# A router inside an attention loop: row normalising moved to ScalarE, and two largest, masks, ranks and sends moved between the slots of a hand-written pipeline

## The chip, the cores and the metric

One core of a Trainium2 chip runs the whole program in one launch. The metric is the device time of an execution in microseconds. The inputs are those of the reference with seed 0, in float32.

## What is computed

Two layers over x of shape (8, 512, 128), each with an adaptive layer norm (shift, scale and gate per sequence). The first has a Mamba-2 mixer and a capacity-limited mixture of experts (here no expert is kept, so its branch isn't entered). The second, whose stages this document is about, is attention with one head and then a router with 8 experts:

```python
mod = (_silu(L1_c) @ L1_wmod).reshape(L1_c.shape[0], 6, 1, -1)
...
h = _layernorm(x) * (1 + ca) + sa
x = x + ga * _L1_attn_ref(h, ...)
h = _layernorm(x) * (1 + cb) + sb
x = x + gb * _L1_ffn_ref(h, ...)

def _L1_ffn_ref(tgt, Wr, br, W1, b1, W2, b2, gamma, beta):
    logits = jnp.einsum('bsd,ed->bse', tgt, Wr) + br
    top_v, top_i = jax.lax.top_k(logits, 2)
    top_w = jax.nn.softmax(top_v, axis=-1)
    ...
    h = jax.nn.relu(jnp.einsum('bsd,efd->bsef', tgt, W1) + b1)
    o = jnp.einsum('bsef,edf->bsed', h, W2) + b2
    tgt2 = jnp.einsum('bsed,bse->bsd', o, router_w)
    return _layer_norm(tgt + tgt2, gamma, beta)
```

## The kernel before, in words

The program has three parts in time. The mixer of layer 0 runs first. The attention of layer 1 with its router follows, and its first slots run beside the mixer's last. Then 71 tiles of 128 queued rows go through their expert, results are scattered back, and the final norm writes the output. The change touches the second part only.

**Slots.** The 8 sequences are 32 chunks of 128 tokens. Each engine has a function `body(m, b, c, first)` that is called for m from -9 to 37, with b = m // 4 and c = m % 4. What a slot m contains, and in which order, is written out by hand in each engine's body; every engine runs its own list in order, and semaphores tie the lists together. In slot m, TensorE (engine PE in the rows) turns the exponentials of chunk m+1 (L1699), makes the scores of chunk m+3 (L1693) and the product with the values of chunk m (`attend`, L1710). ScalarE (ACT) copies the turned exponentials (L1338) and takes exp of the scores (L1342). VectorE (DVE) takes the row maximum of chunk m+3 (nmx, L1471), the reciprocal (rinv, L1483), adds the result to x (L1493), and takes its statistics (L1496, L1507). Once per sequence come query, key and value products (L1675, L1679, L1685), their evictions (the values with an addition on DVE, L1502, in slots with c = 0) and two small weight products on DVE (wvg and bvg, L1466 and L1467, c = 1).

**The router's way of a pair.** Two chunks are a group; there are 16 groups, and group q ends in slot E = 2q + 1, always odd. A group's way through the engines is spread over later slots:

- slot E: variance plus epsilon (ve_b, DVE L1512), then the power -0.5 on GpSimd (POOL, rs_b, L1287; "the pow" from here on);
- slot E+1: the normalised rows (x - mean) * rs_b, two passes of 128x128 on DVE (L1518);
- slot E+2: TensorE turns them (L1718), ScalarE applies scale and shift (h4, L1361);
- slot E+3: TensorE makes rows and logits (L1725), DVE adds the bias (lg), finds the two largest (top) and their indices (top_i), makes the masks (mk, L1535), their sum (ms), the running counts (base) and the weights (wa, L1545 and after); ScalarE takes exp of the difference (eexp, L1367) and copies the rows out twice (L1370, L1371);
- slot E+4: ranks on TensorE (L1735, L1737), which need ms and base;
- slot E+5: rank plus queue start, times masks, summed to the queue numbers (pos, L1487) on DVE, and the sends: four indirect DMAs per group from POOL (L1265), each of 128 rows.

POOL's body issues the sends of a slot first and the pow of that slot second:

```python
for q, j in scatters_at.get(m, ()):
    ...
    scatter(q, j)
if m in ends_at:
    ...
    wait(pool, "b_ve", q + 1)
    wait(pool, "b_xn", q)
    g.tensor_tensor(rs_b[:, 0:n], ve_b[:, 0:n], k.half_neg[:, 0:n], ALU.pow).then_inc(S["b_rs"], 1)
```

`scatter` waits for the group's numbers (`q_pos`) and weights (`q_w1`). After the last slot a matmul counts the queues, DVE builds the table of tiles (L1556 to L1569), and the experts begin once the table is there and all sends have landed.

Of the kernel before, what the change touches and what calls it, by code (L numbers as in the profile page):

```python
# [10 lines left out]
P = 128  # L11
# [104 lines left out]
def mixer(nc, k, a):  # L116
# [6 lines left out]
    with ExitStack() as rounded:  # L123
# [544 lines left out]
        def tensor_program(pe):  # L668
# [153 lines left out]
            "d_hi", "d_t", "d_bd")] + [("c_cu", 1), ("c_mm", 2), ("c_row_mm", 1), ("c_gate", 5), ("c_rk", 1), ("w_mul", NTAP), ("w_hi", NTAP + 2)]  # L822
# [193 lines left out]
def layer1(nc, k, a, out, mixer_of, kept):  # L1016
# [10 lines left out]
            "q_mr", "q_pos", "q_wa", "q_w0", "q_w1", "q_lg", "f_cnt"))  # L1027
# [4 lines left out]
    with ExitStack() as ctx:  # L1032
# [5 lines left out]
        st_b = sb("st_b", [P, 2, 6]); mv_b = sb("mv_b", [P, 2, NC, 2]); ve_b = sb("ve_b", [P, NC]); rs_b = sb("rs_b", [P, NC])  # L1038
# [104 lines left out]
        for m in range(BEGIN, END):  # L1143
            b, c = m // NC, m % NC
            if c == 0 and seq(b + 1):
                used(("v", b + 1), "u_dve")
            if c == 2 and seq(b + 2):
                used(("q", b + 2), "u_act")
            if c == 3 and seq(b + 2):
                used(("k", b + 2), "u_act")  # L1150
            if m - 2 in ends_at:
                used(("h4", ends_at[m - 2]), "u_act")
            if m - 3 in ends_at:
                used(("row", ends_at[m - 3]), "u_act")
            if m - 4 in ends_at:
                used(("rank", ends_at[m - 4]), "u_dve")
# [9 lines left out]
        totals |= {n: G for n in ("b_ve", "b_rs", "b_xn", "q_diff", "q_exp", "q_ms", "q_mr", "q_pos", "q_wa", "q_w0", "q_w1", "q_lg")}  # L1166
# [11 lines left out]
        def filled(e, key):  # L1178

            wait(e, "u_mm", use[key][0] + 1)  # L1180
# [142 lines left out]
        def _(act):  # L1323
            ac = nc.scalar

            def body(m, b, c, first):
                if m == BEGIN:
                    act.wait_ge(S["aw_in"], 16 * 11)
                    wait(act, "sc_mm", 2)
                    ac.activation(wvT[:], bank[0][:, 0:P], ACT.Copy)  # L1330
                    ac.activation(bvT[:], bank[0][:, P:2 * P], ACT.Copy).then_inc(S["sc_exp"], 1)
                    wait(act, "f_mm", k.ends["conv"])
                    wait(act, "res_x", NB)
                    ac.activation(eexp[:, 0:1], ones[:, 0:1], ACT.Exp)
                n = m + 1
                if chunk(n):
                    wait(act, "p_t", n + 1)
                    ac.activation(pt[:, n % 3, :], bank[5][:], ACT.Copy).then_inc(S["p_act"], 1)  # L1338
                n = m + 3
                if chunk(n):  # L1340
                    wait(act, "sc_max", n + 1)
                    ac.activation(pr[:, n % 3, :], bank[3 + n % 2][:], ACT.Exp, bias=nmx[:, n % 2:n % 2 + 1], accum_out=sm[:, n % 4:n % 4 + 1]).then_inc(S["sc_exp"], 1)  # L1342
                if c == 2 and seq(b + 2):
                    s = b + 2
                    filled(act, ("q", s))
                    if s == 0:
                        wait(act, "a_set", 1)
                    ac.activation(qT[:, s % 2, :], bank_of(("q", s))[:], ACT.Identity, scale=0.125, bias=bq[:]).then_inc(S["u_act"], 1)
                if c == 3 and seq(b + 2):
                    s = b + 2  # L1350
                    filled(act, ("k", s))
                    ac.activation(kT[:, s % 2, :], bank_of(("k", s))[:], ACT.Identity, bias=k.attn_b[:, 1:2]).then_inc(S["u_act"], 1)
                if m - 2 in ends_at:
                    q = ends_at[m - 2]
                    s, _, n = groups[q]
                    filled(act, ("h4", q))
                    if q >= 2:
                        filled(act, ("row", q - 2))
                    elif first:
                        wait(act, "s_yz", NT)  # L1360
                    ac.activation(h4[:, q % 2, 0:n * P], bank_of(("h4", q))[:, 0:n * P], ACT.Identity, scale=mod[:, 1, 4, s:s + 1], bias=mod[:, 1, 3, s:s + 1]).then_inc(S["u_act"], 1)  # L1361
                if m - 3 in ends_at:
                    q = ends_at[m - 3]
                    s, c0, n = groups[q]
                    wait(act, "q_diff", q + 1)
                    wait(act, "q_w1", q)
                    ac.activation(eexp[:, 0:n], ediff[:, 0:n], ACT.Exp).then_inc(S["q_exp"], 1)  # L1367
                    filled(act, ("row", q))
                    src = rows_in(q, n)[:, :, 0:P]
                    ac.activation(row[:, s * NC + c0:s * NC + c0 + n, 0, 0:D], src, ACT.Copy)  # L1370
                    ac.activation(row[:, s * NC + c0:s * NC + c0 + n, 1, 0:D], src, ACT.Copy).then_inc(S["u_act"], 1)  # L1371
# [60 lines left out]
        def _(dve):  # L1432
# [8 lines left out]
            def body(m, b, c, first):  # L1441
# [42 lines left out]
                if m - 5 in ends_at:  # L1484
# [35 lines left out]
                if m - 3 in ends_at:  # L1520
                    q = ends_at[m - 3]
# [11 lines left out]
                    wait(dve, "q_at", done)  # L1533
                    for i in range(2):
                        v.tensor_tensor(mk[:, q % 2, i, 0:n], top_i[:, 0:n, i:i + 1].broadcast_to([P, n, NE]), over_chunks(k.iota[:], n), ALU.is_equal).then_inc(S["q_mask"], 1)  # L1535
                    wait(dve, "q_mask", 2 * (q + 1))
                    v.tensor_tensor(ms[:, 0:n], mk[:, q % 2, 0, 0:n], mk[:, q % 2, 1, 0:n], ALU.add).then_inc(S["q_ms"], 1)
                    wait(dve, "q_ms", q + 1)
                    if q == 0:
                        wait(dve, "a_set", 1)  # L1540
                    for i in range(n):
                        wait(dve, "q_base", at + i)
                        v.tensor_tensor(base[:, q % 2, i + 1, :] if i + 1 < n else base[:, (q + 1) % 2, 0, :], base[:, q % 2, i, :], ms[:, i, :], ALU.add).then_inc(S["q_base"], 1)
# [125 lines left out]
        def _(pe):  # L1669
            t_ = nc.tensor  # L1670

            def query(s, first):
                if first and s == 0:
                    wait(pe, "s_aev", k.next_ready[s])
                t_.matmul(bank_of(("q", s))[:], wq, h_next[:, s, :], start=True, stop=True).then_inc(S["u_mm"], 1)  # L1675
# [63 lines left out]
            def body(m, b, c, first):  # L1739
# [24 lines left out]
                if chunk(m + 3):  # L1764
                    scores(m + 3)
                if chunk(m):
                    attend(m)
# [10 lines left out]
                if m - 4 in ends_at:  # L1778
                    ranks(ends_at[m - 4])
# [144 lines left out]
```

## Time and profile before

| | us |
|---|---|
| median of 3 runs | 572.94 (572.18 to 574.33) |
| the profiled execution | 574.9 |
| its span, first to last instruction | 573.0 |
| TensorE busy in the span | 507.9 (89%) |
| DVE busy | 438.5 (77%) |
| ScalarE busy | 352.2 (61%) |
| POOL busy | 280.6 (49%) |

Busy shares are means over the whole program. Matmuls are pipelined and their ends are modelled. POOL's row in the timeline shows an indirect DMA as the time POOL is held by issuing it, not as the transfer. "Idle before" in brackets names what the profile infers as the releaser; a wait for several semaphores is put down to the one that came last by the profile.

### The profile page before, as it was taken

The numbers are of one execution on the slowest core, as the hardware profiler recorded it, in microseconds if no ns is written. First come the engines' busy times: TensorE is split into PE (matmuls) and PEld (weight loads), VectorE is DVE, ScalarE is ACT, GpSimd is POOL, SyncE is SP. The second block draws the span as 40 slices with busy tenths as digits, with TensorE's granted clock in tenths as the row PEclk, the third lists the DMA queues.
The fourth block names the chain that finished last, engine by engine and source line by source line (L and its number), as shares of the span: only waits on it lengthen the run. The fifth ranks groups of instructions, "written<-read, shape, count | busy, mean of one in ns | idle before, by whom it ended". The sixth has DMA issues, their size and how long they took to land.

```text
span 573.0 us, 12147 instructions
## 1 busy us (share of the span) xinstructions
PE 507.9 (89%) x3328; PEld 420.9 (73%) x3328; DVE 438.5 (77%) x1651; ACT 352.2 (61%) x944; POOL 280.6 (49%) x349
## 2 busy tenths in 40 slices
PE   5799999999999999988999999515999999999991
PEld 3467888888888887756777777414999999989630
DVE  3758898989898989977899999853666666656375
ACT  3978787787878584544656666312566666555354
POOL 3144363535353535410266666770666666666323
PEclk9989999999999999999999999855999999999996
DMA  9299999999100000006511111111122222222293
GB/s 279 85 290 176 178 165 179 165 173 185 61 19 15 6 18 2 21 18 194 152 44 39 39 38 44 44 58 45 57 72 68 76 72 68 61 72 67 80 278 112
DMA packets 76386, 54.70 MB, mean 95 GB/s; under 512 B 10524, under 2 KB 69408, under 8 KB 76184
## 3 DMA queue, kind: packets, MB, share of 16 engines
q1 hardware_dynamic: 70352, 43.39, 38.4%
q0 software_dynamic: 4320, 8.99, 4.7%
q10 hardware_dynamic: 1640, 1.45, 0.8%
q8 instruction: 32, 0.52, 0.4%
q14 instruction: 42, 0.34, 0.2%
HBM read 40.62 MB, written 31.58 MB: 126 GB/s over the span
## 4 chain that ended last, share of the span: by engine, by line
PE 62%; DVE 22%; ACT 6%; issue 5%; DMA 2%; DVEq 1%; SPq 0%; POOL 0%; ACTq 0%
PE bank L1817 10%; PE bank L1834 10%; PE bank L678 5%; PE bank L680 5%; PE bank L679 5%; PE bank L789 4%; DVE nmx L1471 2%; PE bank L724 2%; PE bank L809 2%; PE bank L735 2%; PE bank L785 2%; PE bank L794 2%; PE bank L1710 2%; PE bank L720 1%; DVE arena L1607 1%
## 5 line engine op out<-in xcount | busy, mean ns | idle before, releaser
L1307 POOL DMA_INDIRECT results<-arena x71 | 74.2, 1045 | 60.6 <-ACT arena L1395 55.7
L1817 PE MATMUL bank<-front,arena 128*128 128x128 f32 x568 | 77.9, 281 | 2.7 <-DVE arena L1607 1.4
L1265 POOL DMA_INDIRECT queue<-arena,pos x64 | 62.6, 979 | 28.1 <-issue 14.1
L1834 PE MATMUL bank<-h_all,front 128*128 x568 | 75.7, 277 | 0.1
L1817 PEld LDWEIGHTS bank<-front,arena 128*128 128x128 f32 x568 | 70.6, 195 | 5.7 <-issue 4.5
L292 POOL TENSOR_TENSOR arena<-arena,half_neg 128x1 f32<-128x1 f32 x32 | 19.7, 616 | 110.2 <-ACT arena L458 110.2
L1834 PEld LDWEIGHTS bank<-h_all,front 128*128 128x128 f32 x568 | 69.6, 193 | 0.3 <-issue 0.2
L1607 DVE COPY arena<-arena 128x516 f32 x71 | 36.6, 515 | 40.4 <-issue 37.3
L1389 ACT ACTIVATE front<-bank 128x128 f32<-128x128 f32 x71 | 19.7, 278 | 60.9 <-PE bank L1810 42.9
L678 PE MATMUL bank<-h_hi,wc_hi 128*128 128x512 f32 x96 | 45.1, 470 | 1.3 <-ACT arena L439 1.3
L1618 DVE TENSOR_SCALAR front<-bank,arena 128x128 f32<-128x128 f32 x142 | 42.8, 342 | 2.9 <-PE bank L1817 2.6
L1408 ACT ACTIVATE front<-bank,arena 128x128 f32<-128x128 f32 x142 | 43.2, 353 | 2.1 <-PE bank L1817 2.1
L1710 PEld LDWEIGHTS bank<-front 128*128 128x128 f32 x256 | 33.4, 192 | 13.9 <-issue 13.4
L679 PE MATMUL bank<-h_hi,wc_lo 128*128 128x512 f32 x96 | 38.9, 405 | 0.0
L514 DVE TENSOR_TENSOR_SCAN arena<-bank,arena 128x512 f32<-128x512 f32 x32 | 38.8, 1213 | 0.0
L680 PE MATMUL bank<-h_lo,wc_hi 128*128 128x512 f32 x96 | 38.7, 404 | 0.0
L1342 ACT ACTIVATE arena<-bank,nmx 128x512 f32<-128x512 f32 x32 | 22.1, 690 | 23.9 <-DVE nmx L1471 22.3
L1395 ACT ACTIVATE arena<-arena 128x128 f32<-128x128 f32 x71 | 28.5, 402 | 13.0 <-DVE arena L1625 5.2
L789 PEld LDWEIGHTS bank<-arena 128*128 128x128 f32 x256 | 33.1, 192 | 2.5
L789 PE MATMUL bank<-arena 128*128 128x64 f32 x256 | 34.1, 262 | 0.0
L1710 PE MATMUL bank<-front 128*128 128x128 f32 x256 | 33.7, 275 | 0.0
L1810 PE MATMUL bank<-ident_wr,arena 128*128 128x128 f32 x71 | 19.9, 280 | 15.1 <-DMA arena<-queue 15.1
(295 smaller groups left out, 1393.1 us busy)
## 6 DMA issues: line engine op xcount, KB each, us to landing
queue<-in_pad_rows SPq DMA_DIRECT2D x8, 2178.0 KB, 34.8
arena<-queue SPq DMA_DIRECT2D x71, 66.0 KB
rows<-mod_rows SPq DMA_DIRECT2D x8, 384.0 KB, 6.3
x_keep<-x SPq DMA_DIRECT2D x8, 256.0 KB, 2.3
arena<-in_w SPq DMA_DIRECT2D x1, 2048.0 KB, 9.1
h_all<-in_w SPq DMA_DIRECT2D x1, 2048.0 KB, 7.9
h_all<-results SPq DMA_DIRECT2D x8, 256.0 KB, 4.8
arena<-results SPq DMA_DIRECT2D x8, 256.0 KB, 5.2
```

The lines of the kernel that those rows point to most:

```text
L678: t_.matmul(dst, l_hi, r_hi, start=first, stop=False)
L679: t_.matmul(dst, l_lo, r_hi, start=False, stop=False)
L680: return t_.matmul(dst, l_hi, r_lo, start=False, stop=last)
L789: mm = t_.matmul(bank[5][:, h * HD:h * HD + HD], mt[:, t % 2, h * P:h * P + P], xdt[:, t % 2, h * HD:h * HD + HD], start=False, stop=True, ...
L1265: pool.indirect_dma_start(k.queue, bass.IndirectOffsetOnAxis(ap=pos[:, s, i, c0 + j:c0 + j + 1], axis=0), row[:, s * NC + c0 + j, i, :], N ...
L1307: pool.indirect_dma_start(k.results, bass.IndirectOffsetOnAxis(ap=xg[:, c, D:D + 1].bitcast(I32), axis=0), yw[:, c, :], None).then_inc(S[f ...
L1408: ac.activation(ht[:, p, g * P:g * P + P], bank[2 + p][:, g * P:g * P + P], ACT.Relu, bias=wc[:, p, FF + g:FF + g + 1]).then_inc(S["ht_a"], 1)
L1607: v.tensor_copy(wc[:, p, :], w1[:, e, :]).then_inc(S["w_cp"], 1)
L1618: v.tensor_scalar(ht[:, p, g * P:g * P + P], bank[6 + p][:, g * P:g * P + P], wc[:, p, FF + g:FF + g + 1], 0.0, ALU.add, ALU.max).then_inc ...
L1710: mm = t_.matmul(bank[6 + n % 2][:, 0:D], pt[:, n % 3, i * P:i * P + P], vv[:, s % 2, i, :], start=(i == 0), stop=(i == NC - 1))
L1817: mm = t_.matmul(bank[(2 if g < NG // 2 else 6) + p][:, g * P:g * P + P], wc[:, p, g * P:g * P + P], xt[:, p, :], start=True, stop=True)
L1834: mm = t_.matmul(bank[4 + p][:, 0:D], ht[:, p, g * P:g * P + P], w2[:, e, g, :], start=(g == 0), stop=(g == NG - 1))
```

## The change

Every step of a group's way from slot E+1 on changes its place, its engine, or both:

- the normalised rows are made on ScalarE, at the end of slot E+1, as x * rs_b + nm_b; DVE makes nm_b = -mean * rs_b for it in the same slot, right behind the row maximum;
- TensorE turns the rows in slot E+2 as before, but ahead of `attend`, and makes rows and logits at the end of that same slot E+2, not in E+3;
- DVE adds the bias and finds the two largest and the indices in slot E+2 (before E+3), and makes masks, ms and base early in slot E+3 (before: late in E+3) and the weights at its end;
- on ScalarE, eexp comes first in slot E+3, h4 and the copies behind the copy of the turned exponentials;
- ranks move from E+4 to E+3, numbers and sends from E+5 to E+4;
- the loop has one slot less, the new semaphore takes another retired one's place, and the list `use`, by which three PSUM banks go round, follows the new order.

The diff, cut to what the text speaks of:

```diff
         for q, (s, c0, n) in enumerate(groups):
             for j in range(n):
-                at = max(at + (1.0 if n == NC else 0.75), end_of[q] + 5)
+                at = max(at + 0.75, end_of[q] + 4)
                 scatters_at.setdefault(int(at), []).append((q, j))
-        BEGIN, END = -9, NT + 6
+        BEGIN, END = -9, NT + 5
...
         # ScalarE
+                if m - 3 in ends_at:
+                    q = ends_at[m - 3]
+                    n = groups[q][2]
+                    wait(act, "q_diff", q + 1)
+                    wait(act, "q_w1", q)
+                    ac.activation(eexp[:, 0:n], ediff[:, 0:n], ACT.Exp).then_inc(S["q_exp"], 1)
                 n = m + 1
                 if chunk(n):
                     wait(act, "p_t", n + 1)
                     ac.activation(pt[:, n % 3, :], bank[5][:], ACT.Copy).then_inc(S["p_act"], 1)
...
+                if m - 1 in ends_at:
+                    q = ends_at[m - 1]
                     s, c0, n = groups[q]
+                    if q >= 1:
+                        filled(act, ("h4", q - 1))
+                    wait(act, "b_nm", q + 1)
+                    for i in range(n):
+                        ins = ac.activation(xn_b[:, i, :], x[:, s * NC + c0 + i, :], ACT.Identity, scale=rs_b[:, i:i + 1], bias=nm_b[:, i:i + 1])
+                    ins.then_inc(S["b_xn"], 1)
...
         # DVE, behind the row maximum
+                if m - 1 in ends_at:
+                    q = ends_at[m - 1]
+                    s, c0, n = groups[q]
+                    wait(dve, "b_rs", q + 1)
+                    v.scalar_tensor_tensor(out=nm_b[:, 0:n], in0=mv_b[:, s % 2, c0:c0 + n].rearrange("p c t -> p (c t)")[:, 0::2], scalar=-1.0, in1=rs_b[:, 0:n],
+                                           op0=ALU.mult, op1=ALU.mult).then_inc(S["b_nm"], 1)
+                if m - 3 in ends_at:
...
+                    for i in range(2):
+                        v.tensor_tensor(mk[:, q % 2, i, 0:n], top_i[:, 0:n, i:i + 1].broadcast_to([P, n, NE]), over_chunks(k.iota[:], n), ALU.is_equal).then_inc(S["q_mask"], 1)
...
-                if m - 5 in ends_at:
-                    q = ends_at[m - 5]
+                if m - 4 in ends_at:
+                    q = ends_at[m - 4]
                     s, c0, n = groups[q]
                     filled(dve, ("rank", q))
...
         # DVE, at the slot's end
-                if m - 1 in ends_at:
-                    q = ends_at[m - 1]
-                    s, c0, n = groups[q]
-                    wait(dve, "b_rs", q + 1)
-                    for i in range(n):
-                        ins = v.tensor_scalar(xn_b[:, i, :], x[:, s * NC + c0 + i, :], mv_b[:, s % 2, c0 + i, 0:1], rs_b[:, i:i + 1], ALU.subtract, ALU.mult)
-                    ins.then_inc(S["b_xn"], 1)
-                if m - 3 in ends_at:
-                    q = ends_at[m - 3]
+                if m - 2 in ends_at:
+                    q = ends_at[m - 2]
...
         # TensorE
                 if chunk(m + 3):
                     scores(m + 3)
+                if m - 2 in ends_at:
+                    hidden_rows(ends_at[m - 2])
                 if chunk(m):
                     attend(m)
...
                 if m - 2 in ends_at:
-                    hidden_rows(ends_at[m - 2])
+                    rows_and_logits(ends_at[m - 2])
                 if m - 3 in ends_at:
-                    rows_and_logits(ends_at[m - 3])
-                if m - 4 in ends_at:
-                    ranks(ends_at[m - 4])
+                    ranks(ends_at[m - 3])
```

POOL's body stands as it was. Its order changes through the table of sends, here at the first groups (rs_b is the pow, queue the sends). Before:

```order
L292 TENSOR_TENSOR arena<-arena,half_neg 128x1
L278 TENSOR_TENSOR arena<-arena,half_neg 128x1 x2
L1277 MEMSET arena 128x64x2
L1287 TENSOR_TENSOR rs_b<-ve_b,half_neg 128x2 x3
L1265 DMA queue<-arena,pos 34816x132 x4
L1287 TENSOR_TENSOR rs_b<-ve_b,half_neg 128x2
```

And in the changed kernel:

```order
L292 TENSOR_TENSOR arena<-arena,half_neg 128x1
L278 TENSOR_TENSOR arena<-arena,half_neg 128x1 x2
L1277 MEMSET arena 128x64x2
L1287 TENSOR_TENSOR rs_b<-ve_b,half_neg 128x2 x2
L1265 DMA queue<-arena,pos 34816x132 x4
L1287 TENSOR_TENSOR rs_b<-ve_b,half_neg 128x2
```

From there on four sends and a pow alternate in both. The sends of group q stand ahead of the pow of group q + 3 before, and ahead of that of group q + 2 in the change; eight sends stand at the end, not twelve.

DVE in the loop before, from a group's numbers (pos) on, in an even slot:

```order
L1487 TENSOR_REDUCE pos<-mr 128x2x2
L1493 SCALAR_TENSOR_TENSOR x<-bank,rinv,x 128x128
L1496 BN_STATS st_b<-x 128x6
L1507 BN_AGGR mv_b<-st_b 128x2
L1518 TENSOR_SCALAR arena<-x,mv_b,rs_b 128x128 x2
L1525 TENSOR_TENSOR lg<-bank,br 128x16
L1528 MAX top<-lg 128x8 x2
L1530 TENSOR_TENSOR ediff<-top 128x2
L1532 MAX_INDEX top_i<-top,lg 128x8 x2
L1535 TENSOR_TENSOR mk<-top_i,iota 128x16 x2
```

And in the changed kernel, from pos, now in an odd slot, into the next even one:

```order
L1521 TENSOR_REDUCE pos<-mr 128x2x2
L1527 SCALAR_TENSOR_TENSOR x<-bank,rinv,x 128x128
L1530 BN_STATS st_b<-x 128x6
L1541 BN_AGGR mv_b<-st_b 128x2
L1546 TENSOR_SCALAR ve_b<-mv_b 128x2
L1552 TENSOR_TENSOR lg<-bank,br 128x16
L1555 MAX top<-lg 128x8 x2
L1557 TENSOR_TENSOR ediff<-top 128x2
L1559 MAX_INDEX top_i<-top,lg 128x8 x2
L1482 TENSOR_REDUCE nmx<-bank 128x1
L1487 SCALAR_TENSOR_TENSOR nm_b<-mv_b,rs_b 128x2
L1495 TENSOR_TENSOR mk<-top_i,iota 128x16 x2
```

The two passes that read rs_b are gone from DVE; in their place nm_b reads it, and masks, x and the rest of the even slot stand behind nm_b.

## Rows read from the trace of the kernel before

**Rows 1.** Windows, all engines: us, busy us (instructions), granted TensorE clock, DMA share, GB/s.
```profile
285.97:356.00 70.03, 66.75 (x419) 50.40 (x417) 64.71 (x344) 42.05 (x109) 46.55 (x51) 1.00 0.12 40
356.00:378.00 22.00, 12.49 (x77) 9.83 (x77) 17.67 (x111) 8.07 (x23) 16.86 (x18) 0.78 0.15 48
378.00:394.00 16.00, 0.92 (x2) 0.36 (x2) 6.19 (x20) 0.47 (x2) 6.71 (x7) 0.50 0.18 51
```

**Rows 2.** Timeline of DVE, two pairs of slots: start us, duration us, line, out<-in.
```profile
303.12 0.19 DVE L1487 TENSOR_REDUCE pos<-mr 128x4 int32<-128x32 f32 x1
...
303.92 0.67 DVE L1502 TENSOR_TENSOR front<-bank,bvg 128x512 f32<-128x512 f32 x1
...
306.08 0.26 DVE L1535 TENSOR_TENSOR mk<-top_i,iota 128x16 f32<-128x16 uint32 x2
...
306.86 0.16 DVE L1545 TENSOR_SCALAR wa<-eexp 128x2 f32<-128x2 f32 x1
...
307.36 0.29 DVE L1466 TENSOR_TENSOR wvg<-wvo,rows 128x128 f32<-128x128 f32 x1
...
307.77 0.68 DVE L1471 TENSOR_REDUCE nmx<-bank 128x1 f32<-128x512 f32 x1
308.37 0.15 DVE L1483 RECIPROCAL rinv<-sm 128x1 f32<-128x1 f32 x1
...
309.28 0.18 DVE L1507 BATCH_NORM_AGGREGATE mv_b<-st_b 128x2 f32<-128x6 f32 x1
...
309.57 0.69 DVE L1471 TENSOR_REDUCE nmx<-bank 128x1 f32<-128x512 f32 x1
...
310.67 0.19 DVE L1487 TENSOR_REDUCE pos<-mr 128x4 int32<-128x32 f32 x1
...
311.57 0.58 DVE L1518 TENSOR_SCALAR arena<-x,mv_b,rs_b 128x128 f32<-128x128 f32 x2
...
317.23 0.19 DVE L1487 TENSOR_REDUCE pos<-mr 128x4 int32<-128x32 f32 x1
```

**Rows 3.** Timeline of POOL, the same stretch; idle time before in brackets.
```profile
304.09 1.03 POOL L1265 DMA_INDIRECT queue<-arena,pos  x1 [0.97 <-DVE x L1493]
...
307.95 0.96 POOL L1265 DMA_INDIRECT queue<-arena,pos  x1 [0.30 <-issue]
309.75 0.72 POOL L1287 TENSOR_TENSOR rs_b<-ve_b,half_neg 128x2 f32<-128x2 f32 x1 [0.84 <-DVE ve_b L1512]
```

**Rows 4.** Timeline of TensorE, the same stretch.
```profile
306.69 0.17 PE L1735 MATMUL bank<-ms,tri_b 128*128 128x16 bf16 x1 [0.30 <-issue]
...
307.17 0.63 PE L1699 MATMUL bank<-ident_wr,arena 128*128 128x128 f32 x4 [0.19 <-ACT front L1338]
307.64 1.02 PE L1693 MATMUL bank<-front 128*128 128x512 f32 x2
```

**Rows 5.** ScalarE's line 366, an affine pass of the same shape.
```profile
L366 ACT ACTIVATE arena<-x,arena x32: 477/486/500, 6.9 to 167.4; 128x128 f32<-128x128 f32 x32
```

**Rows 6.** Timeline: first number row on DVE, and the tail, all engines.
```profile
282.52 0.19 DVE L1487 TENSOR_REDUCE pos<-mr 128x4 int32<-128x32 f32 x1
...
370.67 0.76 POOL L1287 TENSOR_TENSOR rs_b<-ve_b,half_neg 128x2 f32<-128x2 f32 x1
370.96 0.19 DVE L1487 TENSOR_REDUCE pos<-mr 128x4 int32<-128x32 f32 x1
...
389.20 0.20 DVE L1569 CAST tile_at<-tile_r 128x72 int32<-128x72 f32 x1
```

**Rows 7.** Timeline of TensorE at an early stall.
```profile
23.09 0.39 PE L680 MATMUL bank<-h_lo,wc_hi 128*128 128x512 f32 x1
25.89 0.66 PE L762 MATMUL bank<-ident_wr,arena 128*128 128x128 f32 x4 [2.41 <-ACT arena L358]
```

**Rows 8.** Windows after that stall.
```profile
27.00:28.00 1.00, 0.11 (x1) 0.12 (x1) 0.75 (x1) 0.97 (x3) 0.00 (x0) 0.52 0.74 237
33.00:34.00 1.00, 1.00 (x4) 0.77 (x4) 0.47 (x1) 0.59 (x2) 1.00 (x2) 0.57 1.06 421
```

More of the change, by code:

```diff
@@ L1037, in layer1 @@
         st_a = sb("st_a", [P, NC, 6]); mv_a = sb("mv_a", [P, NC, 2]); ve_a = sb("ve_a", [P, NC]); rs_a = sb("rs_a", [P, NC])
-        st_b = sb("st_b", [P, 2, 6]); mv_b = sb("mv_b", [P, 2, NC, 2]); ve_b = sb("ve_b", [P, NC]); rs_b = sb("rs_b", [P, NC])
+        st_b = sb("st_b", [P, 2, 6]); mv_b = sb("mv_b", [P, 2, NC, 2]); ve_b = sb("ve_b", [P, NC]); rs_b = sb("rs_b", [P, NC]); nm_b = sb("nm_b", [P, NC])
         front = k.front
@@ L1151, in layer1 @@
             if m - 2 in ends_at:
-                used(("h4", ends_at[m - 2]), "u_act")
+                used(("row", ends_at[m - 2]), "u_act")
             if m - 3 in ends_at:
-                used(("row", ends_at[m - 3]), "u_act")
-            if m - 4 in ends_at:
-                used(("rank", ends_at[m - 4]), "u_dve")
+                used(("rank", ends_at[m - 3]), "u_dve")
             if m == 2:
@@ L1338, in body @@
                     ac.activation(pt[:, n % 3, :], bank[5][:], ACT.Copy).then_inc(S["p_act"], 1)
+                if m - 2 in ends_at:
+                    q = ends_at[m - 2]
+                    s, _, n = groups[q]
+                    filled(act, ("h4", q))
+                    if q >= 2:
+                        filled(act, ("row", q - 2))
+                    elif first:
+                        wait(act, "s_yz", NT)
+                    ac.activation(h4[:, q % 2, 0:n * P], bank_of(("h4", q))[:, 0:n * P], ACT.Identity, scale=mod[:, 1, 4, s:s + 1], bias=mod[:, 1, 3, s:s + 1]).then_inc(S["u_act"], 1)
+                if m - 3 in ends_at:
+                    q = ends_at[m - 3]
+                    s, c0, n = groups[q]
+                    src = rows_in(q, n)[:, :, 0:P]
+                    ac.activation(row[:, s * NC + c0:s * NC + c0 + n, 0, 0:D], src, ACT.Copy)
+                    ac.activation(row[:, s * NC + c0:s * NC + c0 + n, 1, 0:D], src, ACT.Copy).then_inc(S["u_act"], 1)
                 n = m + 3
@@ L1471, in body @@
                     v.tensor_reduce(nmx[:, n % 2:n % 2 + 1], bank[3 + n % 2][:], AX.X, ALU.max, negate=True).then_inc(S["sc_max"], 1)
-                if m - 5 in ends_at:
-                    q = ends_at[m - 5]
+                if m - 1 in ends_at:
+                    q = ends_at[m - 1]
+                    s, c0, n = groups[q]
+                    wait(dve, "b_rs", q + 1)
+                    v.scalar_tensor_tensor(out=nm_b[:, 0:n], in0=mv_b[:, s % 2, c0:c0 + n].rearrange("p c t -> p (c t)")[:, 0::2], scalar=-1.0, in1=rs_b[:, 0:n],
+                                           op0=ALU.mult, op1=ALU.mult).then_inc(S["b_nm"], 1)
+                if m - 3 in ends_at:
+                    q = ends_at[m - 3]
+                    s, c0, n = groups[q]
+                    at, done = s * NC + c0, s * NC + c0 + n
+                    wait(dve, "q_at", done)
+                    for i in range(2):
+                        v.tensor_tensor(mk[:, q % 2, i, 0:n], top_i[:, 0:n, i:i + 1].broadcast_to([P, n, NE]), over_chunks(k.iota[:], n), ALU.is_equal).then_inc(S["q_mask"], 1)
+                    wait(dve, "q_mask", 2 * (q + 1))
+                    v.tensor_tensor(ms[:, 0:n], mk[:, q % 2, 0, 0:n], mk[:, q % 2, 1, 0:n], ALU.add).then_inc(S["q_ms"], 1)
+                    wait(dve, "q_ms", q + 1)
+                    if q == 0:
+                        wait(dve, "a_set", 1)
+                    for i in range(n):
+                        wait(dve, "q_base", at + i)
+                        v.tensor_tensor(base[:, q % 2, i + 1, :] if i + 1 < n else base[:, (q + 1) % 2, 0, :], base[:, q % 2, i, :], ms[:, i, :], ALU.add).then_inc(S["q_base"], 1)
+                if m - 4 in ends_at:
+                    q = ends_at[m - 4]
                     s, c0, n = groups[q]
@@ L1483, in body @@
                     v.reciprocal(rinv[:, n % 2:n % 2 + 1], sm[:, n % 4:n % 4 + 1]).then_inc(S["p_rinv"], 1)
-                if m - 5 in ends_at:
+                if m - 4 in ends_at:
+                    q = ends_at[m - 4]
+                    s, c0, _ = groups[q]
                     wait(dve, "q_mr", q + 1)
@@ L1532, in body @@
                         v.max_index(top_i[:, i, :], top[:, i, :], lg4[:, i, :]).then_inc(S["q_at"], 1)
[L1533 to L1543, printed above, removed]
+                if m - 3 in ends_at:
+                    q = ends_at[m - 3]
+                    s, c0, n = groups[q]
+                    at, done = s * NC + c0, s * NC + c0 + n
                     wait(dve, "q_exp", q + 1)
```

30 lines of the change are left out of this document (8 added, 22 removed).

## The prediction, made before the changed kernel had run

> **What bounds the kernel now.** The windows come first [rows 1], because shares of the whole span hide the stages. From 286 to 356 us, the attention loop, TensorE is busy 66.75 of 70.03 us and DVE 64.71; the rest of DVE is pieces of some 0.04 us between dependent instructions. Then, from 356 to 394 us, TensorE runs dry (12.49 of 22.00 us, then 0.92 of 16.00): this is the router's tail, its last groups, the sends that are left, the tile table.
>
> The timelines say who sets the pace of the loop. DVE goes from one pair of slots to the next without a real wait; four slots take 14.11 us from the queue numbers at 303.12 to those at 317.23 [rows 2]. TensorE waits for DVE at one place per four slots, the rank matmul and what follows it, 0.30 and 0.19 us [rows 4]. So DVE bounds the loop and TensorE is 0.5 us behind.
>
> The third reading decides the case: POOL [rows 3]. A group's four sends start 0.78 us after its queue numbers end (303.31 to 304.09), run back to back at 1.26 us, and end at 308.91, 4.82 us later. POOL executes in order. The next pow (line 1287) waits behind them, and here costs nothing: it starts at 309.75, when DVE's variance is ready, and ends at 310.47, while DVE asks for it at 311.57 [rows 2]. The sends fit into the stretch between a group's numbers, early in an even slot, and the variance, late in the odd slot after it.
>
> **The change part by part.**
>
> *Sends and pow on POOL.* Numbers and sends move from the fifth slot after a group's end to the fourth. Groups end in odd slots, so the fourth is odd too, and it is the slot of the pow of the group two further on. POOL's body issues sends first and pow second. The order of POOL says so: two pows and not three ahead of the first four sends. And on DVE the first reader of that pow is now the shift nm_b, right behind the row maximum of the next slot, ahead of the masks, of x and of everything that TensorE waits for. Behind pos stand four sends on POOL, and on DVE only some 2.4 us of work before nm_b (worked out below). That closes a ring once per pair of slots:
> - pos to pow ready: 0.78 + 4.82 + 0.05 (issue) + 0.72 = 6.37 us [rows 3].
> - rest of the even slot from nm_b: nm_b 0.16 (taken as the small pass at 306.86), masks, sum and base 0.78 (306.08 to 306.86), weights 0.50 (to 307.36), reciprocal to aggregate 0.91 (308.37 to 309.28) and 0.10 until the next: 2.45 us [rows 2].
> - the odd slot until pos ends: 309.57 to 310.86, 1.29 us [rows 2].
>
> Sum 10.11 us. With the values' addition (0.67, some 0.6 of it its own) and the two weight products (307.36 to 307.77, 0.41) it is 11.1 in one pair of two. Four slots: 21.2 us instead of 14.1. DVE's own work in them is 14.11 less 0.4 a pair (below), 13.3 us, of which 2 x (2.45 + 1.29) + 1.0 = 8.5 is in the ring; the other 4.8, 2.4 a pair, lies between pos and nm_b beside POOL's 6.37. So DVE stands 3.9 to 4.0 us at nm_b in each pair.
>
> From the first pos to the fourteenth are 13 such steps: 13 x 10.11 = 131.4, plus five values 3.0, plus four weight products 1.6, less two slots without a row maximum 1.2: 134.8 us. Before, that was 370.96 - 282.52 = 88.4 us [rows 6]. **+46.4.**
>
> *The start.* The first pos comes a slot sooner. An odd slot's maximum starts 1.80 us ahead of the next even slot's (307.77 and 309.57 [rows 2]), and two groups' normalising, some 0.5 us each on DVE, is gone from in front of it: **-2.8.**
>
> *The tail.* In the trace the last pow ends at 371.43, 0.28 us after the fourteenth pos (371.15) [rows 6]. Now it stands behind four sends, at +6.37: 6.1 later. What follows it is the old chain with the same links: rows, turning, affine pass, logits, two largest, masks, ranks, numbers, table, to 389.40. Only its first link is slower, see next. Of the eight sends that are left, the first starts some 3 us behind that pow (nm_b, masks and numbers of group 14, 2.2, and 0.78), so they end near 3 + 8 x 1.26 = 13 us; the table ends at 389.40 - 371.43 = 18.0, and stays last unless a send takes over 4 us to land. **+6.4.**
>
> *Normalising on ScalarE.* Two DVE passes of 0.58 us together [rows 2] become two on ScalarE; the nearest row there, same shape, from x with scale and shift, shows 0.49 each [rows 5]: 0.35 us more in the link, counted in the tail. In the loop ScalarE is busy 42.05 of 70.03 us [rows 1] and all of it lies beside POOL's sends. If that cover were gone it would matter: ScalarE gets 0.97 us more per pair and h4, copies and weights in another order, up to 0.9 us for a pair if the rows came after TensorE wants them. The Trainium skill (ScalarE: Activation LUTs, Rules for kernel authors) says to do products and sums on VectorE, not on ScalarE, which speaks against this part. By that rule each of 16 pairs would be dearer, 16 x 0.35 = 5.6 us; by the rows it is a price in the last pair alone.
>
> *What DVE saves.* 0.50 us of normalising less 0.1 of nm_b and a shorter wait at the masks, 0.4 to 0.5 us per pair, is what the change frees where DVE bounds. DVE does not bound any more: the saving is in the ring already and else only lengthens the standing at nm_b. TensorE's moves (turning before attend, logits a slot sooner, ranks a slot sooner) each issue the same matmuls; their waits fall into the 3.9 us too.
>
> Sum without the clock: 46.4 - 2.8 + 6.4 = **+50.0 us.**
>
> *TensorE's clock.* It is at 2.4 GHz throughout the loop now [rows 1]. With 6.7 us of work in 10.1 or 11.1, TensorE gets a gap of 3.4 to 4.4 us per pair, ahead of the ranks. A gap of that size is in the trace: matmuls end at 23.48, 0.66 us of them come at 25.89 [rows 7], and the granted clock of 27 to 28 us is 0.52, half; it is back within 33 to 34 us [rows 8]. A fall costs where matmuls are in the ring: after the masks, DVE's remaining 2.0 us of the even slot and TensorE's ranks, turning and scores (307.17 to 308.66, 1.49 us [rows 4]) are level, so at half clock the odd slot's maximum is 1.5 us late; in the pair with values and weight products 1.0 us of that is covered. After a fall the slow matmuls fill the next gap, so I take every second one, the longer: six or seven times 1.4 us, **+9 us.** Bounds: 0, and 20 if the clock is low most of the time.
>
> Total +59. The profiled execution took 574.9 us (span 573.0), the median is 572.94; against the median the forecast is 632, and I give 631.
>
> **The rivals.**
> - *The clock stays up.* Same ring; 573 + 50 = **623 us.** For it: TensorE had 12.49 us of work in the 22.00 of 356 to 378, a smaller share than it would have here, and the mean clock was still 0.78 [rows 1]. Against: the fall at 27 us came with 0.66 us of work in the gap.
> - *The clock falls in every gap and stays low.* At half clock TensorE's 13.4 us of work per four slots need up to 26.8, more than the ring's 21.2; then TensorE is the bound for part of the loop: 14 pairs at +1.4 or more, **645 us**, up to 655. The Trainium skill (TensorE: Matmul & The Clock Gate, Part 1) says that the throttled state is the default and that an idle TensorE goes back to it; by that rule each of these gaps would end at half clock. The row at 27 us agrees; whether 3.4 us are enough no row shows.
> - *The other side: POOL does not hold the pow.* If the pow reached DVE before nm_b, the change would do what its parts suggest: DVE free of 0.4 us a pair, TensorE the bound, its 3.3 us in 70 [rows 1] coming back over the whole loop, some 4, and a tail a slot shorter, 2 to 3: **567 us.** It decides by one duration: with 2.4 us of DVE's work between pos and nm_b, and 0.78, 0.05 and 0.72 taken anyway, the four sends would have to hold POOL for some 0.9 us in all, not 4.82 [rows 3]. Nothing in the trace shows a pow overtaking a send.
>
> **How the numbers follow.** Forecast, ring with the clock falling in about half of the gaps: 0.52. Clock up: 0.22. Clock low throughout: 0.19. POOL not in the way: 0.05. Something else, mostly an error in the ring's links: 0.02. The range takes the first two whole, with 4 us for the links (each step of the ring is summed thirteen times, so 0.3 us in a step is 4 us), and most of the third: 618 to 650. About 0.5% (3 us) is what a measurement here can tell from no change. Faster 0.05, same 0.01, slower 0.94.
>
> **What would show it.** POOL: each pow directly behind a send, with no wait for DVE. DVE: fourteen idle times of 3 to 4.5 us ahead of the nm_b line, released by POOL. Four slots 21 us apart at pos; the stretch from first to fourteenth pos 135 us or some more. Granted clock of the loop under 1.00, 0.5 in patches. Experts and last stage unchanged. It is wrong if nm_b does not wait, if the time is under 600, or if the pairs exceed 12 us with the clock up.

## The result, and the profile after

| | before | after |
|---|---|---|
| median, us (beside each other on one chip, 4 runs each) | 573.63 (572.18 to 575.03) | 626.92 (625.88 to 627.95) |
| ratio | | 1.0937 [1.0907, 1.0968] |
| span of the profiled execution, us | 573.0 | 626.0 |
| mean granted clock | 0.958 | 0.932 |

Slower by 53 us, where 58 (631 us) was forecast; 618 to 650 holds it. Windows of the changed kernel, all engines, same columns as [rows 1]:

```profile
285.97:400.00 114.03, 80.05 (x418) 58.75 (x418) 62.19 (x337) 53.19 (x130) 48.62 (x53) 0.85 0.08 26
400.00:420.00 20.00, 12.45 (x68) 10.45 (x68) 9.82 (x59) 7.54 (x20) 9.03 (x10) 0.81 0.07 24
420.00:450.00 30.00, 9.98 (x42) 8.15 (x43) 15.47 (x80) 5.84 (x17) 12.98 (x14) 0.58 0.16 45
```

The first window holds as many TensorE instructions (418) as the 70.03 us of [rows 1] (419), and takes 114. TensorE, the busiest, works for 70% of it: the loop has become a chain of waits. POOL's timeline says which chain; it answers to [rows 3]:

```profile
327.59 1.03 POOL L1265 DMA_INDIRECT queue<-arena,pos  x1 [5.83 <-DVE x L1527]
...
331.46 0.96 POOL L1265 DMA_INDIRECT queue<-arena,pos  x1 [0.31 <-issue]
332.44 0.73 POOL L1287 TENSOR_TENSOR rs_b<-ve_b,half_neg 128x2 f32<-128x2 f32 x1
339.00 1.03 POOL L1265 DMA_INDIRECT queue<-arena,pos  x1 [5.82 <-DVE pos L1521]
```

The pow has no idle time in front of it: it stands directly behind the fourth send. POOL then idles 5.8 us, because the next numbers need that pow. DVE in the same stretch (compare [rows 2]):

```profile
326.62 0.19 DVE L1521 TENSOR_REDUCE pos<-mr 128x4 int32<-128x32 f32 x1
...
328.76 0.67 DVE L1482 TENSOR_REDUCE nmx<-bank 128x1 f32<-128x512 f32 x1
333.20 0.16 DVE L1487 SCALAR_TENSOR_TENSOR nm_b<-mv_b,rs_b 128x2 f32<-128x2 f32 x1 [3.77 <-POOL rs_b L1287]
...
336.93 0.69 DVE L1482 TENSOR_REDUCE nmx<-bank 128x1 f32<-128x512 f32 x1 [1.32 <-PE bank L1714]
338.03 0.19 DVE L1521 TENSOR_REDUCE pos<-mr 128x4 int32<-128x32 f32 x1
339.13 0.35 DVE L1527 SCALAR_TENSOR_TENSOR x<-bank,rinv,x 128x128 f32<-128x128 f32 x1 [0.92 <-PE bank L1731]
...
344.61 0.16 DVE L1487 SCALAR_TENSOR_TENSOR nm_b<-mv_b,rs_b 128x2 f32<-128x2 f32 x1 [1.95 <-POOL rs_b L1287]
```

From pos to nm_b it is 6.58 us in both pairs (326.62 to 333.20, 338.03 to 344.61), whatever DVE does in between. The waits of all engines from 262 to 450 us (total, times, longest) show the same wait handed on, from POOL to DVE to TensorE and ScalarE; they overlap and must not be added:

```profile
PE bank L1756 <- DVE ms L1497: 51.2, 15, 5.5
DVE nm_b L1487 <- POOL rs_b L1287: 45.6, 15, 4.4
...
ACT arena L1381 <- DVE nm_b L1487: 33.0, 14, 3.5
```

Last TensorE, at two pairs that stand behind each other (compare [rows 4]):

```profile
333.89 0.17 PE L1756 MATMUL bank<-ms,tri_b 128*128 128x16 bf16 x1 [3.49 <-DVE ms L1497]
...
334.10 1.08 PE L1720 MATMUL bank<-ident_wr,arena 128*128 128x128 f32 x4
334.98 1.92 PE L1714 MATMUL bank<-front 128*128 128x512 f32 x2
...
345.29 0.17 PE L1756 MATMUL bank<-ms,tri_b 128*128 128x16 bf16 x1 [1.58 <-DVE ms L1497]
...
345.50 0.63 PE L1720 MATMUL bank<-ident_wr,arena 128*128 128x128 f32 x4
345.96 1.02 PE L1714 MATMUL bank<-front 128*128 128x512 f32 x2
```

After 3.49 us of idle time the scores take 1.92 us, nearly twice their 1.02: the granted clock is 0.50 there, which is the lower of its two levels, 1.2 GHz. That is where DVE's row maximum is 1.32 us late (336.93 above). After 1.58 us of idle time they take 1.02 as before. But the idle time just ahead of the masks doesn't decide alone, as two more pairs show:

```profile
322.49 0.17 PE L1756 MATMUL bank<-ms,tri_b 128*128 128x16 bf16 x1 [2.11 <-DVE ms L1497]
...
323.57 1.91 PE L1714 MATMUL bank<-front 128*128 128x512 f32 x2
...
367.45 0.17 PE L1756 MATMUL bank<-ms,tri_b 128*128 128x16 bf16 x1 [2.39 <-DVE ms L1497]
...
368.12 1.02 PE L1714 MATMUL bank<-front 128*128 128x512 f32 x2
```

From the first to the fourteenth pos the clock falls in nine of thirteen such gaps, three times in pairs that follow each other (312, 322 and 332 us), so not simply in every second one. Behind seven of the nine stand scores and more; the last two, at 411 and 421 us, have no scores behind them.

### The profile page after: what moved, and what is told of

Read it like the earlier page. It is cut to its first block and busy times, and to the rows that moved or that the text cites. A ratio compares the mean times of both kernels' runs of the same rounds, so it can differ in the third digit from the quotient of the medians.

```text
span 626.0 us, 12179 instructions
## 1 busy us (share of the span) xinstructions
PE 524.8 (84%) x3328; PEld 433.5 (69%) x3328; DVE 433.2 (69%) x1635; ACT 368.2 (59%) x976; POOL 281.6 (45%) x349
## 5 line engine op out<-in xcount | busy, mean ns | idle before, releaser
L1756 PE MATMUL bank<-ms,tri_b 128*128 128x16 bf16 x16 | 2.7, 170 | 51.2 <-DVE ms L1497 51.2
L1731 PEld LDWEIGHTS bank<-front 128*128 128x128 f32 x256 | 39.2, 227 | 7.7 <-issue 6.7
L1756 PEld LDWEIGHTS bank<-ms,tri_b 128*128 128x128 bf16 x16 | 1.6, 100 | 57.1 <-issue 57.1
L1731 PE MATMUL bank<-front 128*128 128x128 f32 x256 | 40.2, 309 | 0.0
L1714 PE MATMUL bank<-front 128*128 128x512 f32 x64 | 39.0, 698 | 0.0
```

The lines of the kernel that those rows point to most:

```text
L1714: t_.matmul(bank[3 + n % 2][:], qT[:, s % 2, i * P:i * P + P], kT[:, s % 2, :], start=True, stop=True).then_inc(S["sc_mm"], 1)
L1731: mm = t_.matmul(bank[6 + n % 2][:, 0:D], pt[:, n % 3, i * P:i * P + P], vv[:, s % 2, i, :], start=(i == 0), stop=(i == NC - 1))
```

## The experiments

The theory: the ring pos, four sends, pow, nm_b, closed by POOL's order and by the place of nm_b on DVE. Its rivals: other parts of the change (ScalarE's rows, TensorE's order), or the clock as the main cause. "Before" stands for the kernel before on the same chip, 570.27 us unless said otherwise.

**The pow ahead of the sends.** POOL's body in the changed kernel, nothing else touched:

```diff
-                for q, j in scatters_at.get(m, ()):
...
-                    scatter(q, j)
                 if m in ends_at:
...
                     g.tensor_tensor(rs_b[:, 0:n], ve_b[:, 0:n], k.half_neg[:, 0:n], ALU.pow).then_inc(S["b_rs"], 1)
+                for q, j in scatters_at.get(m, ()):
...
+                    scatter(q, j)
```

> The changed kernel, with the pow ahead of the sends in POOL's body and nothing else. Theory (ring through POOL: numbers, four sends, pow, nm_b): the pow no longer stands behind the sends, so the idle time before nm_b, 45.6 us in all in the changed kernel, falls under 2 us, four slots take 13.2 to 14.1 us, TensorE's clock stays at 1.00 in the loop, and the time is 564 to 573 us. Rival (the moves of TensorE's and ScalarE's steps make the loop slow by themselves, POOL only shows it): the time stays above 600 us.

Measured 569.08 us, ratio 0.9976 [0.9963, 0.9990]. All 53 us are gone by the exchange of two blocks of one engine's program; the rest of the change costs nothing. DVE's idle time at nm_b falls from 45.6 us in all to 0.8. Four slots take 14.07 us. The same window as the first of [rows 1]:

```profile
285.97:356.00 70.03, 66.82 (x420) 49.23 (x418) 60.95 (x335) 51.88 (x132) 46.55 (x51) 1.00 0.12 40
```

DVE has 3.8 us less to do than in [rows 1], and TensorE does as much in the same time: DVE's saving is real, but buys next to nothing (the total is 1.2 us under the kernel before). More on this below.

**Sends a slot later.** The other way to get the sends behind the pow:

```diff
-                at = max(at + 0.75, end_of[q] + 4)
+                at = max(at + 0.75, end_of[q] + 5)
```

> The changed kernel, with the sends back in the fifth slot after a group's end (an even slot) and nothing else moved. Theory of the ring: as with the pow first, since the pow of the odd slot stands ahead of these sends: no idle time before nm_b, 564 to 573 us. Rival (the moves on the other engines): above 600 us.

Measured 569.53, ratio 0.9989 [0.9976, 1.0002]. Again the loss is gone, with POOL's body as it stands. In the slot table or in the body, it is the order of sends and pow that counts.

**The kernel before with the sends in E+4**, and nothing else of the change:

```diff
-                at = max(at + (1.0 if n == NC else 0.75), end_of[q] + 5)
+                at = max(at + (1.0 if n == NC else 0.75), end_of[q] + 4)
```

> The kernel before, with only the sends a slot sooner (they then wait on POOL for numbers that DVE makes in the next slot). Theory of the ring: numbers to normalising on DVE takes 6.6 us from start to start instead of 0.90, so a pair takes 7.05 + 5.7 = 12.8 us, 13 pairs +74 us, with the tail and some low clock 645 to 670 us: slower than the changed kernel. Rival (ScalarE's and TensorE's new order costs the time): near 573 us.

Measured 653.89, ratio 1.1464 [1.1427, 1.1502]. That one digit alone makes the kernel before slower than the changed one: there the numbers are made in E+5 still, so POOL stands at the first send until then, and the pow behind the four reaches the normalising at the end of that same slot late. Nearly all of two slots of DVE's work is in the ring, and a pair takes 13.08 us, where 12.8 was expected; the granted clock from 286 to 356 us is 0.77. Its largest wait on DVE, from 262 to 470 us, is at the normalising line, the pow's first reader there:

```profile
DVE arena L1518 <- POOL rs_b L1287: 70.2, 14, 6.4
```

**Half of the sends behind the pow.** Of a group's four, numbered j, each two get a slot of their own:

```diff
-                at = max(at + 0.75, end_of[q] + 4)
+                at = end_of[q] + 4 + j
```

> The changed kernel with a dose: two of each group's four sends stay ahead of the pow (fourth slot), two go to the fifth slot, behind it. Theory of the ring: numbers to nm_b falls from 6.58 to 6.58 - 2.52 = 4.06 us, the idle time before nm_b from some 3.3 to 1 to 1.5 us per pair, four slots take some 16 us: 583 to 592 us. Rival (any send ahead of the pow costs the whole stall): above 610 us.

Measured 585.98, ratio 1.0266 [1.0229, 1.0303]. DVE's waits at nm_b shrink from 45.6 to 14.2 us in all:

```profile
DVE nm_b L1487 <- POOL rs_b L1287: 14.2, 11, 2.0
```

Up to the twelfth pos a pair takes 8.3 us on average (7.5 to 9.1), more than the 7.05 before and less than the 11 of the changed kernel. So the loss grows with the sends ahead of the pow: 569, 586 and 627 us with none, two and four. That it starts once they are longer than what DVE has to do meanwhile is what the ring says; no run with one send shows it.

**The ring without the clock.** Ten unused 128x128 products per group on TensorE, ahead of the wait for the masks, so that the gap is filled (their results are read by nobody):

```diff
                 bank_free(pe, ("rank", q))
+                for _ in range(10):
+                    t_.matmul(bank_of(("rank", q))[:, P:2 * P], ident[:], ident[:], start=True, stop=True)
                 wait(pe, "q_ms", q + 1)
```

> The changed kernel with ten 128x128 matmuls of no use ahead of each group's rank matmul, into a free part of the rank's own PSUM bank, in the gap in which TensorE waits. Theory (some 7 of the 141.6 us from the first to the fourteenth queue numbers are TensorE at half clock): granted clock of the loop at 1.00, that stretch 134 to 137 us, the time 619 to 623 us. Rival (the clock costs nothing, the ring's links are longer than summed): the same or slower, 626 to 632 us.

Measured 624.25 (before: 572.78), ratio 1.0916 [1.0881, 1.0950]. The window of the loop and both kinds of pair on TensorE:

```profile
285.97:400.00 114.03, 98.91 (x663) 80.17 (x662) 64.86 (x354) 56.61 (x138) 49.26 (x55) 0.97 0.08 27
```
```profile
331.97 0.18 PE L1758 MATMUL bank<-ms,tri_b 128*128 128x16 bf16 x1 [2.16 <-DVE ms L1497]
...
332.74 1.02 PE L1714 MATMUL bank<-front 128*128 128x512 f32 x2
...
342.82 1.02 PE L1714 MATMUL bank<-front 128*128 128x512 f32 x2
```

The clock is up (0.97, these scores 1.02 us), and the loss is nearly all still there. From first to fourteenth pos it is 135.2 us, where the changed kernel needs 141.6: at least 6.4 us of its 53 are the clock's. The filler doesn't keep the clock up everywhere. It falls at 375 and at 395 us, and again in the last of these pairs, at 416. At 395:

```profile
394.94 0.18 PE L1758 MATMUL bank<-ms,tri_b 128*128 128x16 bf16 x1 [2.35 <-DVE ms L1497]
...
395.81 1.92 PE L1714 MATMUL bank<-front 128*128 128x512 f32 x2
```

The pairs with the falls at 375 and 395 take 10.59 and 11.09 us, most others of their kind 10.1 (with the values' addition and the weight products 10.87). Without these two falls the stretch would be 133.7 us and the clock's share 7.9 us, an estimate from these pairs.

The median is 1.25 us over the 619 to 623 that were expected, and little of the 6.4 us is seen in the total: each kernel against the kernel before on its own chip, the loss is 51.5 us and was 53.3, with intervals that overlap. In the profiled executions the span is 4.0 us shorter (622.0 and 626.0). The stretch gives 6.4 back, but the first pos comes 0.9 later, and from the fourteenth pos to the end of the table it is 20.6 us and not 18.9.

**nm_b later on DVE.** POOL's order stays as changed; DVE's block of nm_b goes from behind the row maximum to the end of the same slot:

```diff
                     v.tensor_reduce(nmx[:, n % 2:n % 2 + 1], bank[3 + n % 2][:], AX.X, ALU.max, negate=True).then_inc(S["sc_max"], 1)
-                if m - 1 in ends_at:
...
-                    v.scalar_tensor_tensor(out=nm_b[:, 0:n], ...
...
+                if m - 1 in ends_at:
...
+                    v.scalar_tensor_tensor(out=nm_b[:, 0:n], ...
                 if m - 2 in ends_at:
```

> The changed kernel, POOL's order untouched (sends ahead of the pow), but nm_b on DVE at the end of slot E+1 and not behind its row maximum: the ring is the same, and the even slot's 2.45 us of DVE's work lies beside POOL's sends instead of behind them. By the ring's links: pos to pow ready 6.37, nm_b 0.15 and 0.1, the odd slot until pos 1.29: 7.9 to 8.0 us a pair, with the weight products 16.2 per four slots, first to fourteenth pos 105, idle time ahead of nm_b 1.3 to 1.8 us a pair; total 584 to 590. If the place of the reader did not matter: 11 us a pair and 627.

Measured 594.04, ratio 1.0431 [1.0406, 1.0456]. More than half of the loss (53 us, here 24) goes by the place of the reader alone, but four slots take 16.87 us, not 16.2, and the total is 4 us over what was expected. DVE's timeline over two pairs, and POOL's two pows:

```profile
315.34 0.19 DVE L1515 TENSOR_REDUCE pos<-mr 128x4 int32<-128x32 f32 x1
...
321.91 0.16 DVE L1545 SCALAR_TENSOR_TENSOR nm_b<-mv_b,rs_b 128x2 f32<-128x2 f32 x1 [1.40 <-POOL rs_b L1287]
321.99 0.16 DVE L1565 TENSOR_SCALAR wa<-eexp 128x2 f32<-128x2 f32 x1
...
323.56 0.19 DVE L1515 TENSOR_REDUCE pos<-mr 128x4 int32<-128x32 f32 x1
...
324.62 0.35 DVE L1521 SCALAR_TENSOR_TENSOR x<-bank,rinv,x 128x128 f32<-128x128 f32 x1 [0.88 <-PE bank L1731]
...
330.13 0.16 DVE L1545 SCALAR_TENSOR_TENSOR nm_b<-mv_b,rs_b 128x2 f32<-128x2 f32 x1
...
332.22 0.19 DVE L1515 TENSOR_REDUCE pos<-mr 128x4 int32<-128x32 f32 x1
```
```profile
321.15 0.73 POOL L1287 TENSOR_TENSOR rs_b<-ve_b,half_neg 128x2 f32<-128x2 f32 x1
...
329.37 0.73 POOL L1287 TENSOR_TENSOR rs_b<-ve_b,half_neg 128x2 f32<-128x2 f32 x1
```

From pos to nm_b it is 6.57 us in both pairs (in the changed kernel 6.58): each nm_b starts 0.03 us after its pow ends (321.88 and 330.10). From nm_b to the next pos it is 1.65 us in the one pair and 2.09 in the other, which has the weight products. So the ring is complete in both, 8.21 and 8.66 us. The expectation left out a term of it: DVE's three passes for the weights (wa and what follows, 321.99 to 322.46) now stand behind nm_b at the end of the even slot. They take some 0.3 us more of each pair than was summed, 0.6 of the 0.67 us that four slots are over. In the second pair nm_b shows no idle time, because DVE, held up by 0.88 us at x, is done with its own work just as the pow ends.

**A second profile of the kernel before.**

> The kernel before, unchanged, for a second profile. In its first profile DVE needs 8.7 us for the table of tiles (380.67 to 389.40) and shows idle time between dependent small instructions there (1.18, 0.63, 1.48, 0.64 us); the changed kernel and four variants show 5.7 to 6.0 us. If the gaps belong to that one execution: table 5.7 to 6.0 us here, last pow to table end 13 us instead of 18.0, four slots still 14.1 us, time 570 to 573. If they belong to the code of the kernel before: 8.7 us again.

The time was 571.09, span 569.2, four slots 14.05 (6.53 and 7.51 a pair). DVE's timeline, from the last numbers into the table:

```profile
378.11 0.18 DVE L1487 TENSOR_REDUCE pos<-mr 128x4 int32<-128x32 f32 x1
378.22 0.41 DVE L1556 TENSOR_TENSOR over<-bank,tile_rows 128x256 f32<-128x256 f32 x1
378.67 0.42 DVE L1558 TENSOR_REDUCE tiles<-over 128x8 f32<-128x256 f32 x1
379.12 0.17 DVE L1559 TENSOR_TENSOR_SCAN ends<-ones,tiles 128x8 f32<-128x8 f32 x1
379.33 0.17 DVE L1560 TENSOR_SCALAR skip<-tiles 128x8 f32<-128x8 f32 x1
```

And the same in the first profile:

```profile
380.67 0.41 DVE L1556 TENSOR_TENSOR over<-bank,tile_rows 128x256 f32<-128x256 f32 x1
381.71 0.42 DVE L1558 TENSOR_REDUCE tiles<-over 128x8 f32<-128x256 f32 x1 [0.63 <-DVE over L1556]
382.17 0.17 DVE L1559 TENSOR_TENSOR_SCAN ends<-ones,tiles 128x8 f32<-128x8 f32 x1
383.82 0.23 DVE L1560 TENSOR_SCALAR skip<-tiles 128x8 f32<-128x8 f32 x1 [1.48 <-DVE ends L1559]
```

Idle times of 0.63 and 1.48 us between neighbours stand in the first profile only. The table takes 6.0 us and not 8.7, and from the end of the last pow to the end of the table it is 12.7 us and not 18.0. So the gaps are not the kernel's own. (The second profile comes from another chip, on which the kernel before takes 570.27 us and not 573.63; the changed kernel has no such gaps in its profile either.)

**Where DVE's saving went.** Four runs, three of them on the form with the pow first. In the first the rows go back to DVE:

```diff
-                    v.scalar_tensor_tensor(out=nm_b[:, 0:n], ...
...
-                        ins = ac.activation(xn_b[:, i, :], ...
...
+                        ins = v.tensor_scalar(xn_b[:, i, :], x[:, s * NC + c0 + i, :], mv_b[:, s % 2, c0 + i, 0:1], rs_b[:, i:i + 1], ALU.subtract, ALU.mult)
```

In the second, `ranks` on TensorE moves behind the scores of the next slot:

```diff
                 if chunk(m + 3):
                     scores(m + 3)
+                if m - 4 in ends_at:
+                    ranks(ends_at[m - 4])
...
-                if m - 3 in ends_at:
-                    ranks(ends_at[m - 3])
```

In the last two TensorE has less to do: the product with the values leaves out the last 128 keys of a sequence, in the form with the pow first and in the kernel before.

```diff
-                for i in range(NC):
-                    mm = t_.matmul(..., stop=(i == NC - 1))
+                for i in range(NC - 1):
+                    mm = t_.matmul(..., stop=(i == NC - 2))
```

> The changed kernel with the pow ahead of the sends, and the normalised rows back on DVE at the end of slot E+1, without nm_b. Prices the move to ScalarE where POOL is out of the way. DVE gets 2 x 0.58 - 2 x 0.15 = 0.86 us more per four slots. If DVE's time still counts: four slots 14.5 to 14.9 us and 572 to 575. If TensorE bounds (it waits only some 0.6 us in 14.07 with the rows on ScalarE): 14.1 to 14.3 and 569 to 571. ScalarE 0.97 us less per pair either way.

> The changed kernel with the pow ahead of the sends, and the rank matmuls one slot later on TensorE, behind that slot's scores; DVE reads them at the same place. TensorE then never waits for the masks (0.31 us per four slots there). If what is left of the loop's four slots (14.07) over TensorE's own 13.5 comes from TensorE and DVE waiting for each other at masks and ranks: 13.6 to 13.8 us, 566 to 568. If it comes from elsewhere (the turned exponentials, the rows from ScalarE): 14.0 and 569. The tail is set by POOL's last sends and can eat 1 us of it.

> The changed kernel with the pow ahead of the sends, and with only three of the four value matmuls of a chunk on TensorE (the last 128 keys are left out of the product). Takes some 0.2 to 0.25 us from every slot on TensorE, 0.8 to 1.0 per four slots, and nothing from DVE. If TensorE bounds this loop: four slots 13.1 to 13.3 us instead of 14.07, first to fourteenth pos shorter by 5 to 6 us. If the loop is held by waits in a circle with DVE and ScalarE, only a part: 13.6 to 13.9. If DVE bounds it: 14.0.

> The same cut (three of the four value matmuls of a chunk) in the kernel before. The prediction said that DVE bounds that loop and TensorE is 0.5 us per four slots behind: then four slots stay 14.0 to 14.1 us. If TensorE bounds it in truth: 13.1 to 13.3.

| | four slots, us | median, us | ratio |
|---|---|---|---|
| pow first | 14.07 | 569.08 | 0.9976 [0.9963, 0.9990] |
| and rows on DVE | 14.4 | 571.25 | 1.0024 [1.0002, 1.0045] |
| and ranks later | 14.1 | 569.02 | 0.9977 [0.9963, 0.9992] |
| and one value product of four less | 13.84 | 566.4, one run | |
| before, one value product of four less | 14.06 | 571.03, one run (before: 571.41) | |

The last row agrees with a step of the prediction: the kernel before doesn't get shorter when TensorE has less to do, so TensorE doesn't bound it. That DVE does is argued, since no run takes work from DVE alone there. With the pow first, neither engine alone does. Some 0.9 us less on TensorE give 0.23, 0.86 more on DVE cost 0.3 (this run falls between its two expectations). Later ranks give nothing. The largest waits of TensorE from 283 to 353 us, with the pow first and then with later ranks:

```profile
PEld bank L1756 <- ACT arena L1359: 5.5, 5, 1.1
PEld bank L1739 <- ACT front L1369: 5.3, 5, 1.1
```
```profile
PEld bank L1739 <- ACT front L1369: 4.9, 5, 1.0
PE bank L1739 <- ACT arena L1381: 4.6, 5, 0.9
```

The wait in front of the ranks (L1756) is gone, and one for ScalarE's rows (L1381) has come at their turning (L1739), while the period stays. This fits a circle of waits over TensorE, DVE and ScalarE of 14.07 us, about the old 14.05 to 14.11; its links weren't traced, so it isn't shown. The rows on ScalarE save 0.3 us per four slots against the rows on DVE, where DVE is spared 0.86.

## Why the prediction was right

- **POOL executes in order, and sends(q) stand ahead of pow(q+2): right.** Shown by the two kernels that only restore the order (569 us both) and by the kernel before with that order alone (654).
- **pos to pow ready 6.37 us: right.** Measured 6.58 from the start of pos to the start of nm_b, which is 0.19 for pos and 6.39.
- **Pairs of 10.11 and 11.1, 134.8 us to the fourteenth pos: right without the clock** (10.1, 10.87, 135.2 with the filler). That the sums agree within 0.4 us is partly luck: the pairs with the values are 0.2 us shorter than summed, and two falls of the clock, 1.5 us by the estimate above, fill this up. With the clock as it is, the changed kernel's pairs are mostly 10.9 and 11.4 us, 141.6 in all for 143.8 (134.8 and 9).
- **DVE stands 3.9 to 4.0 us at nm_b in each pair: right in every second pair** (3.77 to 4.41). In the others it is 1.80 to 3.20 up to the twelfth, as the slow matmuls take up to 1.7 us of the same cover (the idle times at x, lg and nmx sum to 0.92 + 0.44 + 0.37 between 338.03 and 344.61).
- **The clock falls in about half of the gaps, six or seven times 1.4 us, 9 us: right, the size a little high.** Seven falls have scores behind them, two more have none. Together they cost at least 6.4 us, 7.9 by the estimate above, which is 1.1 a fall. The Trainium skill (TensorE: Matmul & The Clock Gate, Part 1) says that an idle TensorE goes back to the throttled state. The trace agrees for the idle times of 3.49 us and more ahead of the masks, each of which ends at half clock; below that it goes both ways (2.11 us yes, 2.39 and 1.58 no).
- **The start, -2.8: the sign right.** The first pos comes at 281.49 for 282.52 in the first profile and 283.08 in the second, 1.0 or 1.6 sooner and not 2.8.
- **The tail, +6.4: measured +0.7.** From the end of the fourteenth pos to the end of the table it was 371.15 to 389.40, 18.2 us, and is 18.9. This is the term that failed, and the link was not the reason: the last pow is 6.37 behind pos as said. What follows it is 12.6 us for 18.0, since the idle times among DVE's small instructions are missing. Against the second profile the stretch grows from 13.8 to 18.9, +5.1. The size of 18.0 us was taken from the first profile alone: the prediction took them as the chain's own, though DVE's timeline there showed idle time that no other engine ended.
- **Normalising on ScalarE: costs nothing, right, and more.** With POOL out of the way it is the better place by 2.2 us (571.25 and 569.08). The rule of the Trainium skill (ScalarE: Activation LUTs, Rules for kernel authors) would have it on VectorE; here, where VectorE is busy for 63.0 of 70 us with the rows and ScalarE for 43.6, the runs say otherwise.
- **The rival "POOL does not hold the pow", 567 us**, does not hold for the changed kernel, but the form with the pow first is what it describes. That gave 569.08, 1.2 us less than the kernel before where the rival had 6: the loop gives back 0.4 of the 4 us that the rival counted on (first to fourteenth pos 86.8 us for the 87.2 of the second profile).

The sum against the second profile (span 569.2): start -1.6, first to fourteenth pos 141.6 for 87.2, +54.4; tail +5.1; experts and last stage 183.8 for 185.0, -1.2. Together 56.8, which is what the spans differ by. That is more than the measured 53.3, since the second profile comes from the chip on which the kernel before is faster; against the first profile the parts are -1.0, +53.2, +0.7 and +0.2, together 53.0 (span 573.0).

## What to carry to other kernels

Before a step of a hand-written pipeline is moved, write down for each in-order queue that it passes what stands behind it and who needs that first; here a send of 1.26 us, harmless in one slot, cost 53 us one slot sooner, and one exchange of blocks gave it back. When a ring can be closed, sum its links: the sum was within 0.4 us of 135 here, with some luck, and most pairs within 0.2 us of theirs. And read a chain's length from two profiled executions, or take out idle time that waits for nothing, before it goes into a sum.

## What the runs showed that was not expected

In one execution of the kernel before, DVE's dependent small instructions have idle times of 0.3 to 1.5 us between them, some 5 us within 10; in a second profile of the same program, and in those of the changed kernel and ten variants, the table is built without them (5.6 to 6.1 us). What they are the records don't say. And a gap of TensorE that halves its clock costs less than the slowed matmuls: the scores are 0.9 us longer after each such gap, but a part of what follows lies beside POOL's sends, and 6.4 to 7.9 us in 141.6 remain for seven falls with scores behind them.
